# Window attention block on one core: rows before weights, and a first batch with its own order on DVE and Pool

## The reference

```python
h = _ln(win, ln1_g, ln1_b)
q, k, v = h @ wq + bq, h @ wk + bk, h @ wv + bv            # 3 heads of 32
attn = softmax(q k^T / sqrt(32))                           # within a window of 64 tokens
win = win + (attn v) @ wo + bo
h2 = _ln(win, ln2_g, ln2_b)
win = win + gelu(h2 @ w1 + b1) @ w2 + b2                   # 96 -> 384 -> 96
```

## Time and profile before

| | us |
|---|---|
| median of 3 runs | 5156.3 (5153.09 to 5162.12) |
| profiled execution | 5161.67, its span 5159.6 |
| TensorE busy | 4931.7 (96%) |
| DVE busy | 4066.8 (79%) |
| ACT busy | 3875.7 (75%) |
| Pool busy | 3610.9 (70%) |
| scores of step 0, 1 and 12 of the first batch | 54.36, 85.81, 207.08 |
| first MLP product of the first batch | 251.39 |

### The profile page before, as it was taken

How to read it: one execution, slowest core, us unless ns; L and a number is a source line. 1 busy time by engine, 2 the same in 40 slices (tenths; PEclk the granted TensorE clock), 3 DMA queues, 4 the chain that set the end, 5 groups by cost and what they waited for, 6 DMA issues and landing times.

```text
span 5159.6 us, 275615 instructions
## 1 busy us (share of the span) xinstructions
PE 4931.7 (96%) x103124; PEld 4152.4 (80%) x103124; DVE 4066.8 (79%) x9254; ACT 3875.7 (75%) x8206; POOL 3610.9 (70%) x3549
## 2 busy tenths in 40 slices
PE   5999999999999999999999999999999999999999
PEld 4788878888888888888888888888888878888887
DVE  7968878698786977869778697786978879688786
ACT  5949679596785968859588695876949769496794
POOL 5776767776676766767667676776776767767676
PEclk9999999999999999999999999999999999999999
DMA  3042230422313133131321313223142230422304
GB/s 103 19 123 67 76 107 25 120 63 81 103 32 119 58 89 97 39 117 49 101 85 51 114 40 111 76 63 109 35 119 70 67 108 26 125 65 76 107 25 122
DMA packets 222029, 410.68 MB, mean 80 GB/s; under 512 B 29225, under 2 KB 131850, under 8 KB 221898
## 3 DMA queue, kind: packets, MB, share of 16 engines
q1 hardware_dynamic: 221896, 409.55, 26.7%
q10 hardware_dynamic: 2, 0.00, 0.0%
HBM read 208.11 MB, written 201.33 MB: 79 GB/s over the span
## 4 chain that ended last, share of the span: by engine, by line
PE 60%; DVE 10%; SPq 10%; issue 8%; DMA 6%; ACT 2%; POOL 2%; DVEq 1%; ACTq 0%; POOLq 0%
PE psum L552 14%; PE psum L567 7%; PE psum L598 7%; PE psum L627 6%; PE psum L678 6%; PE psum L584 6%; PE psum L613 6%; SPq L283 5%; DMA oT<-turned_rows 5%; PE psum L664 5%; PE psum L520 4%; DVE normed L956 3%; SPq L289 3%; DVE normed L963 2%; DVE normed L973 2%
## 5 line engine op out<-in xcount | busy, mean ns | idle before, releaser
L354 POOL TENSOR_TENSOR probs<-probs,prob_inv 128x512 f32<-128x512 f32 x771 | 783.1, 1043 | 857.3 <-DVE prob_inv L936 857.3
L726 ACT ACTIVATE normed<-stream,shift,rstd 128x96 f32 (+1 forms) x2072 | 770.6, 460 | 42.1 <-POOL shift L402 22.9
L942 DVE TENSOR_TENSOR stream<-stream,psum 128x384 f32 x1024 | 547.3, 549 | 296.0 <-PE psum L678 215.1
L892 DVE BATCH_NORM_STATS2 stats<-stream 128x6 f32 (+2 forms) x4224 | 716.3, 243 | 50.9 <-DVE stream L942 33.0
L393 POOL TENSOR_TENSOR rstd<-variance,minus_half 128x8 f32<-128x8 f32 (+3 forms) x197 | 743.5, 3774 | 15.4
L361 POOL TENSOR_TENSOR hT<-hT_upper,hT_lower 96x1024 f32<-96x1024 f32 x258 | 614.1, 2380 | 11.4 <-DVE hT_lower L905 5.7
L928 DVE TENSOR_REDUCE prob_sum<-probs 128x8 f32<-128x512 f32 x771 | 494.5, 678 | 92.4 <-ACT probs L760 92.2
L806 ACT ACTIVATE gelu_odd<-psum 128x512 f32<-128x512 f32 x768 | 424.0, 592 | 180.4 <-PE psum L664 157.9
L678 PEld LDWEIGHTS psum<-w_w,gelu_odd 128*64 128x64 f32 x12288 | 511.9, 137 | 59.0 <-issue 59.0
L815 ACT ACTIVATE h2T_odd_upper<-oT 96x512 fp32r<-96x512 f32 x224 | 129.0, 623 | 566.2 <-DMA oT<-turned_rows 566.2
L920 DVE TENSOR_TENSOR probs<-psum,row_max 128x512 f32<-128x512 f32 x771 | 532.9, 691 | 26.6
(11 more groups left out here) (94 smaller groups left out, 11318.0 us busy)
## 6 DMA issues: line engine op xcount, KB each, us to landing
turned_rows<-normed SPq DMA_DIRECT2D x624, 128.0 KB
stream<-in_x SPq DMA_DIRECT2D x272, 192.0 KB, 3.1
out<-stream SPq DMA_DIRECT2D x256, 192.0 KB
stream<-in_x SPq DMA_DIRECT2D x272, 180.0 KB
out<-stream SPq DMA_DIRECT2D x256, 180.0 KB
probsT<-turned_rows SPq DMA_DIRECT2D x112, 384.0 KB, 3.2
oT<-turned_rows SPq DMA_DIRECT2D x112, 384.0 KB, 3.3
turned_rows<-gelu_odd SPq DMA_DIRECT2D x144, 128.0 KB
```

The source lines that it names most:

```text
L354: nc.gpsimd.tensor_tensor(block_h, block_h, inv, ALU.mult).then_inc(probs_ready, 1)
L726: last = nc.scalar.activation(normed1[:, t, :], stream[:, slot, t * C:(t + 1) * C], ACT.Identity, bias=shift1[:, index, t:t + 1], scale=rs ...
L892: last = nc.vector.bn_stats(stats[:, index, c, :], stream[:, slot, c * C:(c + 1) * C])
L942: nc.vector.tensor_tensor(part, part, psum[:, banks[g], 0:GROUP], ALU.add).then_inc(added, 1)
```

## The change

The 15 weight transfers are no longer issued by SP ahead of the rows, but by ACT, ahead of `bo`. DVE takes the statistics of units 0 and 1 before it waits for the weights, and writes the constant rows of the MLP's halves only between the attention's steps -2 and -1. The first batch's attention is taken out of the loops of DVE and Pool and written out with its own order: DVE takes the statistics of one unit per step (unit 7 + s after step s, for s up to 10, and unit 18 after step 12), Pool finishes two units at a time, in every second step. The MLP of the first batch stands outside the loop too, with the finish of units 6 and 7 in it; batches 1 to 15 keep their order.

```diff
 @block.sync
-            for i, w in enumerate((wq, wk, wv)):
-                sp.dma_start(qkv_raw[:, i, :], w.rearrange("c h d -> c (h d)")).then_inc(weights_in, 16)
-            for i, b in enumerate((bq, bk, bv)):
-                sp.dma_start(bias_rows[ONES:ONES + 1, i * C:(i + 1) * C],
-                             b.rearrange("(a h) d -> a (h d)", a=1)).then_inc(weights_in, 16)
...
-            sp.dma_start(wo_w[0:C, :], wo.rearrange("h d c -> (h d) c")).then_inc(weights_in, 16)
 @block.gpsimd
-            pool.wait_ge(consts_set, 4)
-            finish1(0, 0, 0, AHEAD)
-            unite_hT(0)
-            finish1(1, AHEAD, AHEAD, LN_GROUP)
-            unite_hT(1)
-            normalise_probs(0, 0)
-            finish1(2, 7, 7, LN_GROUP)
-            finish1(3, 11, 11, LN_GROUP)
-            finish1(4, 15, 15, 1)
+            def first_attention():
+                calls = iter(range(FIRST_CALLS))
+                pool.wait_ge(consts_set, 4)
+                finish1(next(calls), 0, 0, 1)
+                finish1(next(calls), 1, 1, 1)
+                unite_hT(0)
+                finish1(next(calls), 2, 2, 2)
+                unite_hT(1)
+                normalise_probs(0, 0)
+                finish1(next(calls), 4, 4, 2)
+                for s in range(BATCH):
+                    unite_hT(s + 2)
+                    if s in (1, 3, 5, 7, 9):
+                        finish1(next(calls), s + 5, s + 5, 2)
+                    if s == 2:
+                        finish2(next(calls), 0, 0, 2)
+                    if s in (4, 6, 10):
+                        n = (4, 6, 10).index(s)
+                        normalise2(0, n, n)
+                    if s == 8:
+                        finish2(next(calls), 2, 2, 2)
+                    if s == 11:
+                        finish1(next(calls), BATCH, 0, 2)
+                    if s in (12, 14):
+                        n = (s - 12) // 2
+                        lower_early(0, n, n, copy_h2T_early(n, n))
+                    if s == 13:
+                        finish1(next(calls), BATCH + 2, 2, 1)
+                    if s == 15:
+                        finish2(next(calls), 4, 4, 2)
+                    normalise_probs(s + 1, (s + 1) % 2)
+                return next(calls)
...
+            def mlp(b, call, first):
...
+                    if first and j == 0:
+                        finish2(call, batch + 6, 6, 2)
+                        call = call + 1
...
+            mlp(0, first_attention(), True)
+            with batches(mybir.EngineType.Pool, 1) as b:
+                mlp(b, attention(b), False)
 @block.scalar
+            for i, w in enumerate((wq, wk, wv)):
+                act.dma_start(qkv_raw[:, i, :], w.rearrange("c h d -> c (h d)")).then_inc(weights_in, 16)
...
+            act.dma_start(wo_w[0:C, :], wo.rearrange("h d c -> (h d) c")).then_inc(weights_in, 16)
             act.sem_inc(gelu_done, GELU_AHEAD)
             act.wait_ge(rows_cleared, 5)
             act.dma_start(wo_w[ONES:ONES + 1, :], bo.rearrange("(a n) -> a n", a=1)).then_inc(weights_in, 16)
 @block.vector
+            def first_statistics(n):
+                statistics1(n, n % BATCH, n // 2, n % 2)
+
+            first_statistics(0)
+            first_statistics(1)
             dve.wait_ge(weights_in, 16 * (N_WEIGHT_DMAS + 1))
...
-            for upper, lower in (hT_split, *h2T):
+            def constant_rows(upper, lower):
                 nc.vector.tensor_copy(upper[C:P, :], oT[C:P, :])
                 nc.vector.tensor_tensor(lower[C:P, :], oT[C:P, :], oT[C:P, :], ALU.subtract)
+
+            constant_rows(*hT_split)
...
-            for u in range(AHEAD):
-                statistics1(u, u, u // 2, u % 2)
-            for u in range(-AHEAD, 0):
-                attention_step(u, u % 2)
-                if u == -AHEAD:
-                    for n in range(AHEAD, AHEAD + LN_GROUP):
-                        statistics1(n, n, n // 2, n % 2)
-            for n in range(AHEAD + LN_GROUP, BATCH):
-                statistics1(n, n, n // 2, n % 2)
+            first_statistics(2)
+            first_statistics(3)
+            attention_step(-3, 1)
+            first_statistics(4)
+            first_statistics(5)
+            attention_step(-2, 0)
+            first_statistics(6)
+            for halves in h2T:
+                constant_rows(*halves)
+            attention_step(-1, 1)
+
+            TURNS = (5, 8, 11)
+
+            def first_attention():
+                for s in range(BATCH):
+                    attention_step(s, s % 2)
+                    statistics2(s, s)
+                    if s <= 10:
+                        first_statistics(7 + s)
+                    if s == 12:
+                        first_statistics(BATCH + 2)
+                    if s in TURNS:
+                        n = TURNS.index(s)
+                        turn_h2(n, turned_early, n == 0)
...
+            first_attention()
+            mlp(0)
+            with batches(mybir.EngineType.DVE, 1) as b:
+                attention(b)
+                mlp(b)
```

94 lines of the change are left out of this document (47 added, 47 removed).

## The result

| | before | after |
|---|---|---|
| median, us | 5157.44 (6 runs, 5153.09 to 5163.98) | 5119.77 (6 runs, 5112.97 to 5127.18) |
| ratio | | 0.9924, 95% interval 0.9914 to 0.9934 |
| profiled execution, its span | 5161.67, 5159.6 | 5120.26, 5118.4 |

The kernel is faster: by 37.7 us on the median, by 41.4 in the profiled executions.

A forecast was written before the change was run, and what follows sets the result against it. TensorE (96% busy) and its hand-offs bound the body, so the start and first batch were read apart: 30.1 us gained by step 1, less 2.3 paid in eleven steps, 27.8 off 5156.3, about 5129; range 5120 to 5140.

The forecast's parts named there:

- Start: Kernel start: first row issued at 0.75, weights landed at 12.1, TensorE's first transposition at 18.7 instead of 32.13 us.
- A: Weights land at SP's rate, 10.1 us, DVE's extra only 0.5: gain 31.6, time 5125; chance 0.20.
- B: Issues of the two queues hinder each other, weights at 14.4 us: gain 25.5, time 5131; chance 0.18.
- First maximum: First batch, DVE: first maximum at 35.2 us, with 2.5 of the constant rows' 3.6 us back on the path.
- Steps 0 and 1: First batch's attention: scores at 43.1 and 55.7 us, step 0 taking 12.6 instead of 31.45; 30.1 us earlier.
- The 1.4 us set for the clock in step 0: TensorE's V product in step 0 takes half of 2.83 at the upper clock, 1.4 us less.
- Steps 1 to 11: First batch's attention: one statistics per step fills DVE; 123.6 us together, costing 2.3, of it 1.8 for two transpositions.
- Batches 1 to 15 keep their instructions; they start earlier.: The batches after the first: same instructions, only an earlier start; no time gained or lost in the sum.
- Batches of another length: Sign that the prediction is wrong: later batches not lasting as long as before.
- C: DVE becomes the first batch's bound, 6 us, with late weights: 5135, or 5140 if Pool also lags; chance 0.13.
- D: Each of 15 loop iterations of DVE and Pool stalls at its head, the jump from MLP to attention: 5181; chance 0.03.
- E: Step 0: Pool's hT of unit 2 still waits for rows, only 6.3 us won: 5150; chance 0.03.

The follow-up runs named there:

- after_again: The changed kernel run once more, unaltered; 5123.8 us, ratio 0.9925 to the kernel before.
- after_sp_shift15: The changed kernel plus 15 increments of an unused semaphore on SP ahead of its loop over the batches; 5134.2 us, ratio 0.9940 to the kernel before.
- after_sp_shift8: The changed kernel plus 8 increments of an unused semaphore on SP ahead of its loop over the batches; 5133.2 us, ratio 0.9938 to the kernel before.

## Why the prediction was wrong, point by point

- **Start.** Weights at 11.73 (forecast 12.1, between rivals A and B). ACT's 15 issues took 7.8 us, from 0.74 to 8.57, where SP's took 6.3; so an issue on ACT beside SP's cost 0.1 us more, not the 0.27 of the one row; whether the other queue or ACT itself is the reason was not tried apart. SP's first row went out at 0.74. Transposition 18.45 (18.7), Q and K 22.33 (22.7). Right.
- **First maximum.** 36.25 (35.2). The 1.0 is the constant rows: the first copy took 1.72 instead of 0.68, while Pool's hT was at work from 30.45. A first sign of the collision that decides the MLPs; I had priced the rows from a place where Pool was idle.
- **Steps 0 and 1.** Scores at 44.01 (43.1) and 56.58 (55.7): gain 29.2 of the 30.1 forecast. The 1.4 us set for the clock in step 0 was sound: the V product took 2.83 at a granted clock of 0.50 (80.87 to 83.70, before), 1.54 at 1.00 (127.04, before), and 1.88 at 1.00 here; from hT's end (53.08) to the next scores it was 3.5 (3.7).
- **Steps 1 to 11.** Scores of step 12 at 181.07, so 124.5 us (123.6 forecast, 121.3 before). The turns cost what was said: step 5 took 11.86 where step 6 takes 10.89, and DVE is full there, 11.57 of it (columns as in the earlier trace rows):

```profile
113.59:125.45 11.86, 10.92 (x289) 8.98 (x289) 11.57 (x33) 10.93 (x26) 8.40 (x7) 1.00 0.11 34
125.45:136.34 10.89, 10.54 (x289) 8.85 (x289) 10.61 (x31) 10.57 (x24) 10.03 (x15) 1.00 0.12 36
```

  Of the 0.9 above the forecast, the pause of 0.99 in step 1's scores is the likely source: after_again doesn't have it, and takes 123.3 for the eleven steps.
- **First MLP product.** 225.12 (223.6); 223.4 in after_again, 223.0 in after_sp_shift15.
- **The step that failed: "Batches 1 to 15 keep their instructions; they start earlier."** The sum put these batches at nothing. They kept their instructions, but not their time: 14.2 us less in the profile. "Batches of another length" stood among the prediction's own signs of being wrong, and that sign came. Most of it, 11 us, goes with the place of SP's code, by after_sp_shift15, after_sp_shift8 and the table's two groups: without the 15 transfers ahead of them SP's loops lose less time at their branch and the turned units leave 0.3 to 0.4 us sooner. In the changed kernel the 12 MLPs that aren't short gain 0.5 us each; the three short ones, where DVE gets ahead of Pool at unit 11 (before has none), bring the rest, and what makes them short stays open. Put SP's loops elsewhere and what is left is ratio 0.9940 (0.9922 to 0.9958), which from 5156.3 gives 5125, within 5120 to 5140 and a us from the forecast's own range.
- **Rivals.** A and B each held by half. C's full DVE showed in the two turning steps only. D was the nearest to the truth, a price at a jump in all 15 iterations, but I looked for it at DVE's and Pool's outer loop and on the slow side only, and did not ask what the removed instructions move on SP. E did not happen.
- The range took in no effect on the 15 batches (D's 5181 lay outside it); yet 1 us in an MLP, 0.3% of a batch, is 15 us in the sum.

## What to carry to other kernels

"The loop keeps its instructions" doesn't mean that it keeps its time. Where a change adds or removes instructions ahead of a loop on a queue that the loop waits for, a few tenths of a us per pass in either direction belong in the range, times the passes. And where DVE and Pool both work from SBUF, read the spread of one instruction's duration (0.96 to 3.6 here): long Pool operations in one block make DVE lose turn after turn, and cutting three of them into six was worth more (0.65 to 0.72%) than the 26 us, 0.5%, that the new start and order won in the first batch. Cutting two more lost part of it again, so each division has to be measured.

## What the runs showed of the hardware

- From the start of the branch at the end of SP's loop to the next instruction it is 0.16 or 0.29 to 0.33 us with the same loop body, by where the code stands: 8 or 15 instructions ahead of it, and 15 transfers, all made 0.16 into 0.29 or 0.30, and the copies of the loop for batches 15 and 16 have 0.33 and 0.30 beside the 0.16 of the first. On DVE, 1, 2 or 4 instructions ahead of a loop did not move its idle time of 0.28 (four did not move 0.15 in the changed kernel either). Which places are good ones, and why, stays open.
- A DVE operation on 128x768 with two SBUF inputs takes 0.96 alone and up to 3.6 while Pool's operations run. At unit 11 in the changed kernel a start up to 0.17 us behind Pool's shift gave 3.7 to 3.9 us from subtraction to turn, a start 0.53 or more behind it 6.1 to 6.4.
- An execution of a kernel can have MLPs of 137 and of 142 us side by side with the same instructions; the sum over 15 repeats to some us, which MLPs are short doesn't.
